# One core, gated mLSTM and routed experts: last heads spread by matmul, q masked for two sequences at a time, and a new order of the routing

## The reference, cut to what matters

```python
def _mlstm_forward(q, k, v, Wi, bi, Wf, bf, ln_scale):
    ...
    log_D = log_fg + jnp.transpose(ig, (0, 1, 3, 2))
    max_log_D = jnp.max(log_D, axis=-1, keepdims=True)
    D = jnp.exp(log_D - max_log_D)
    qk = jnp.einsum('bhsd,bhtd->bhst', qh, kh) / jnp.sqrt(jnp.asarray(dh, q.dtype))
    C = qk * D
    normalizer = jnp.maximum(jnp.abs(C.sum(-1, keepdims=True)), jnp.exp(-max_log_D))
    Cn = C / (normalizer + EPS)
    h = jnp.einsum('bhst,bhtd->bhsd', Cn, vh)
    mu = h.mean(-1, keepdims=True)
    var = ((h - mu) ** 2).mean(-1, keepdims=True)
    hn = (h - mu) * jax.lax.rsqrt(var + EPS)
    hn = hn * ln_scale.reshape(1, nh, 1, dh)
    return hn.transpose(0, 2, 1, 3).reshape(b, s, e)

def _L0_ffn_ref(hidden_states, w_gate, w1, w3, w2):
    logits = x @ w_gate
    logits = SOFTCAP * jnp.tanh(logits / SOFTCAP)
    probs = jax.nn.softmax(logits, axis=-1)
    _, idx = jax.lax.top_k(probs, TOPK)
    mask = jax.nn.one_hot(idx, E, dtype=probs.dtype).sum(-2)
    weights = probs * mask
    for e in range(E):
        h = jax.nn.silu(x @ w1[e]) * (x @ w3[e])
        out = out + h @ w2[e] * weights[:, e:e + 1]

x = x + jnp.tanh(g_xattn[0]) * _L0_xattn_ref(_layernorm(x), ctx, ctx, Wi, bi, Wf, bf, ln_scale)
x = x + jnp.tanh(g_ffn[0]) * _L0_ffn_ref(_layernorm(x), w_gate, w1, w3, w2)
```

## Time and profile before

| | |
|---|---|
| median of 3 runs | 229.91 us (229.88 to 231.53) |
| the profiled execution's own time | 229.46 us |
| its span, first to last instruction | 227.7 us |
| mean granted TensorE clock | 0.956 of full speed |
| PE busy | 197.8 us (87%) |
| VectorE (DVE) busy | 129.8 us (57%) |
| ScalarE (ACT) busy | 111.9 us (49%) |
| GpSimd (POOL) busy | 88.8 us (39%) |

### The profile page before, as it was taken

One profiled execution on the slowest core, in us unless ns is written; L12 is line 12 of the kernel. 1 busy time (PEld: TensorE's weight loads), 2 busy tenths in 40 slices (PEclk: granted clock), 3 DMA queues, 4 the chain that ended last, 5 costly groups with the idle time before them and its releaser, 6 DMA issues.

```text
span 227.7 us, 4241 instructions
## 1 busy us (share of the span) xinstructions
PE 197.8 (87%) x1331; PEld 146.4 (64%) x1332; DVE 129.8 (57%) x310; ACT 111.9 (49%) x224; POOL 88.8 (39%) x96
## 2 busy tenths in 40 slices
PE   8999899898978712769999999999999999999940
PEld 2488544444436511557888888888888888888830
DVE  6897574679899878976777852223323222222310
ACT  2478888898855795026666622233223322223210
POOL 8100343365740000510445646555444555453222
PEclk9999999999999855699999999999999999999997
DMA  3999999901011140210232233333333322334222
GB/s 117 313 367 376 371 373 374 342 24 49 0 49 46 46 153 33 62 33 1 44 53 46 46 49 46 50 55 61 57 58 42 50 46 46 46 52 62 27 23 23
DMA packets 20032, 23.41 MB, mean 103 GB/s; under 512 B 3888, under 2 KB 15152, under 8 KB 20016
## 3 DMA queue, kind: packets, MB, share of 16 engines
q1 hardware_dynamic: 13696, 16.94, 21.6%
q0 software_dynamic: 4464, 6.16, 17.2%
q10 hardware_dynamic: 1856, 0.10, 0.5%
HBM read 17.95 MB, written 5.24 MB: 102 GB/s over the span
## 4 chain that ended last, share of the span: by engine, by line
PE 74%; DVE 12%; ACT 5%; issue 4%; DMA 2%; POOL 1%; DVEq 0%; POOLq 0%; ACTq 0%
PE bank L1335 28%; PE bank L1352 17%; PE bank L1164 6%; PE bank L1061 4%; PE bank L1344 4%; PE bank L1204 3%; ACT arena L487 2%; PE bank L1317 2%; PE bank L1085 2%; DMA out_dram<-hraw,sidx 2%; PE bank L1180 2%; DVE arena L787 1%; DVE vp L968 1%; PE bank L1184 1%; PE bank L1228 1%
## 5 line engine op out<-in xcount | busy, mean ns | idle before, releaser
L447 POOL DMA_INDIRECT out_dram<-hraw,sidx x23 | 37.6, 1636 | 63.1 <-DVE hraw L1021 57.2
L1335 PE MATMUL bank<-arena_r,xn_sb_r 128*128 x184 | 57.2, 392 | 0.0
L1015 DVE TENSOR_TENSOR x_sb<-x_sb,bank 128x512 f32<-128x512 f32 x23 | 15.8, 688 | 57.5 <-ACT x_sb L637 57.5
L1352 PE MATMUL bank<-w_sb,xn_sb 128*128 x184 | 43.6, 380 | 0.8 <-ACT xn_sb L641 0.8
L1335 PEld LDWEIGHTS bank<-arena_r,xn_sb_r 128*128 128x128 f32 x184 | 34.6, 188 | 7.1
L1335 PE MATMUL bank<-w_sb_r,xn_sb_r 128*128 x92 | 38.2, 415 | 0.8 <-issue 0.6
L637 ACT ACTIVATE x_sb<-bank 128x512 f32<-128x512 f32 x23 | 13.7, 598 | 49.5 <-PE bank L1335 49.5
L1352 PEld LDWEIGHTS bank<-w_sb,xn_sb 128*128 128x128 f32 x184 | 33.2, 190 | 4.6 <-issue 1.0
L408 POOL TENSOR_SCALAR_AFFINE_SELECT arena<-arena 128x1024 f32<-128x1024 f32 x16 | 17.7, 1104 | 36.6 <-ACT arena L517 36.6
L641 ACT ACTIVATE xn_sb<-bank 128x512 f32<-128x512 f32 x23 | 13.7, 598 | 25.8 <-PE bank L1344 25.8
L787 DVE TENSOR_TENSOR arena<-bank,arena 128x1024 f32<-128x1024 f32 x16 | 19.6, 1222 | 7.0 <-POOL arena L408 6.8
(11 more groups left out here) (206 smaller groups left out, 257.8 us busy)
## 6 DMA issues: line engine op xcount, KB each, us to landing
w_sb<-in_L_ffn_w_dram SPq DMA_DIRECT2D x24, 512.0 KB, 9.3
x_sb<-in_x_dram SPq DMA_DIRECT2D x2, 512.0 KB, 6.7
arena<-in_ctx_dram SPq DMA_DIRECT2D x2, 512.0 KB, 9.3
out_dram<-x_sb SPq DMA_DIRECT2D x8, 128.0 KB, 1.8
xnorm_scratch<-xn_sb SPq DMA_DIRECT2D x8, 128.0 KB, 1.7
out_dram<-hraw,sidx POOLq DMA_INDIRECT x23, 3.8
cvT<-xnorm_scratch,gidx POOLq DMA_INDIRECT x12
hraw<-xnorm_scratch,gidx POOLq DMA_INDIRECT x11, 2.9
```

What stands on the lines that cost most here:

```text
L447: nc.gpsimd.indirect_dma_start(out=out[:, :], out_offset=bass.IndirectOffsetOnAxis(ap=sidx[:, i:i + 1], axis=0), in_=y_sb[i % 2], in_offse ...
L1335: last = nc.tensor.matmul(ps_scores[p][:, n, :], a, w, start=(k == 0 and j == 0), stop=(k == KC - 1 and j == 2))
L1352: last = nc.tensor.matmul(ps_tr[:, 0:H], hT_sb[p][:, k * P:(k + 1) * P], w2_sb[:, bass.ds(e * W2 + k * H, H)], start=(k == 0), stop=(k == ...
```

## The change

`mask_q` takes two sequences at a time (16 operations on 128 by 512 in place of 32 on 128 by 256), in the even iterations only. For the last two sequences `turn_cv` multiplies with `to_rows` (the identity with `lns` folded in, 17 columns per head without gaps) in place of transposing with the identity; the squares are taken from cvT (`square_last`), and PE sums them over each head with `in_head` (`spread_last`). The top two are looked for in the capped logits and not in their exponentials; the exponentials of the two values found are taken by ScalarE later (`wtop`). Three of the 16 one-hot rows are made by ScalarE, as relu(1 - |slot - i|), VectorE makes the others in two steps. The selectors of weights and the scatter's indices move behind `lower_x(0, 0)`, `slot_weights` behind `split(1)`, the weight table on PE behind the first tile. Warm-ups with other operands are dropped; two and eight of the ordinary kind are added.

```diff
+        LATE_OH = 3
+        SOME = (0, 8, NS - LATE_OH)
+        sqT = dec[:, 0].rearrange("p h s -> p (h s)").rearrange("p (i n) -> p i n", i=2)
...
-            def mask_q(b, heads):
-
-                act.wait_ge(s_qks, Q_STORED[b // 2])
+            def mask_q(seqs, heads):
+
+                act.wait_ge(s_qks, Q_STORED[seqs[-1] // 2])
+                bs = slice(seqs[0], seqs[-1] + 1)
                 for h in heads:
-                    nc.scalar.activation(qm[:, b, :, h, :], qkT[:, b, 0:KC, :], ACT.Copy,
+                    nc.scalar.activation(qm[:, bs, :, h, :], qkT[:, bs, 0:KC, :], ACT.Copy,
                                          scale=pmask[:, h:h + 1]).then_inc(s_qm, 1)
...
+            def square_last(i):
+                act.wait_ge(s_ots, B - 1 + i)
+                nc.scalar.activation(sqT[:, i, :], cvT[:], ACT.Square).then_inc(s_sqT, 1)
...
-                if b + 2 < B:
-                    mask_q(b + 2, (0, 1))
+                if b % 2 == 0 and b + 2 < B:
+                    mask_q((b + 2, b + 3), (0, 1))
...
+                if b >= B - 2:
+                    square_last(b - B + 2)
+                if b % 2 == 0 and b + 2 < B:
+                    mask_q((b + 2, b + 3), (2, 3))
...
-            square_heads(NG - 1)
...
+            act.wait_ge(s_top, 2)
+            nc.scalar.activation(wtop[:], r8[:, 0:TOPK, :], ACT.Exp, scale=SOFTCAP).then_inc(s_exl, 1)
             nc.scalar.preload_act_table_set("silu_and_others")
+            act.wait_ge(s_dump, 16)
+            act.wait_ge(s_slf, 1)
+            for n in range(LATE_OH):
+                follow(nc.scalar.activation(slotd[n % 2], iota_r[:], ACT.Abs, scale=-1.0, bias=slotf[:, n:n + 1]))
+                nc.scalar.activation(oh_r[:, NS - LATE_OH + n, :], slotd[n % 2], ACT.Relu, scale=-1.0,
+                                     bias=one_c[:, 0:1]).then_inc(s_ohl, 1)
...
                     nc.vector.tensor_scalar(lns[:], lns[:], tg[:, 0:1], None, ALU.mult).then_inc(s_par2, 1)
+                    dve.wait_ge(s_par2, 2)
+                    rows = ident.rearrange("p (j v) -> p j v", v=VW)
+                    nc.vector.tensor_reduce(in_head[:], rows[:, :, 0:DH], AX_X, ALU.add).then_inc(s_scl, 1)
+                    nc.vector.tensor_tensor(to_rows[:, :, :, 0:DH],
...
+                    nc.vector.tensor_copy(to_rows[:, :, :, DH:], rows[:, :, DH:DH + 1].unsqueeze(1).to_broadcast(
...
             center_heads(g)
-            spread_heads(g)
+            dve.wait_ge(s_spr, 1)
+            nc.vector.scalar_tensor_tensor(out=rs[:, 0, :], in0=ps_scores[0][:, 0, 0:NH2], scalar=1.0 / DH,
+                                           in1=s16[:, 2, :], op0=ALU.mult, op1=ALU.add).then_inc(s_var, 1)
             stats_x2(g - 1)
+            finish(g)
             aggregate_x2(g - 1)
-            link(nc.vector.tensor_tensor(hh[:], hraw[:, 2 * g % 4:2 * g % 4 + 2, :, 0:DH],
...
-            finish(g)
-            link(nc.vector.tensor_tensor(hflat, hflat, per_head(rs[:, 1, :]), ALU.mult))
+            link(nc.vector.tensor_tensor(hflat, raw_heads(g), per_head(rs[:, 1, :]), ALU.mult))
...
-            lower_weights(0, 1)
...
-            dve.wait_ge(s_exl, 1)
-            src = ex
+            dve.wait_ge(s_th, 1)
+            src = lt
...
+            nc.vector.tensor_copy(slotf[:], sloti[:, 1, NS - LATE_OH:]).then_inc(s_slf, 1)
...
-            for q in range(4):
...
+            for q in range(2):
...
+            lower_weights(0, 1)
             lower_weights(0, 3)
 
+            dve.wait_ge(s_exl, 2)
...
             lower_x(0, 0)
+            token_slots()
+            select_weights()
+            split(1)
             slot_weights()
-            split(1)
             hidden(0, 0)
...
+                    if b < B - 2:
+                        last = nc.tensor.transpose(ps_h[:, g * P:(g + 1) * P], part, ident[:])
+                    else:
+                        last = nc.tensor.matmul(ps_h[:, g * 4 * (DH + 1):(g + 1) * 4 * (DH + 1)], part,
+                                                to_rows[:, g].rearrange("p j v -> p (j v)"), start=True, stop=True)
...
+            def spread_last():
+
+                for i in range(2):
+                    pe.wait_ge(s_sqT, i + 1)
+                    if i == 0:
+                        pe.wait_ge(s_cm, 2 * B)
+                    for g in range(4):
+                        last = nc.tensor.matmul(ps_scores[0][:, 0, i * NH + 4 * g:i * NH + 4 * g + 4],
+                                                sqT[:, i, g * P:(g + 1) * P], in_head[:], start=True, stop=True)
+                last.then_inc(s_spr, 1)
...
+            spread_last()
             turn_x2(1)
             warm_up(4)
...
             turn_x2(3)
+            warm_up(2)
             logits(3)
...
             last.then_inc(s_tab, 1)
+            warm_up(8)
...
-            warm_up(4)
-            warm_up_r(8, 2 * P)
-            warm_up_r(8, P)
             turn_x(0, s_xg[0], 16, 0)
-            weight_table()
             gate_up(0, 0, expert_of(0), 0)
             turn_x(1, s_xg[1], 16, 1, 1)
+            weight_table()
             turn_h(0, 0, False)
```

More of the change, by code:

```diff
@@ L119, in bass_gated_mlstm_moe_kernel @@
         bmask_r = placed("bmask", [P, B])[1]
+        to_rows = sb("to_rows", [P, 4, 4, DH + 1])
+        in_head = sb("in_head", [P, 4])
         tri_s = sb("tri_s", [P, P], BF16)
@@ L173, in bass_gated_mlstm_moe_kernel @@
         etf = sb("etf", [P, NT])
+        slotf = sb("slotf", [P, LATE_OH])
+        wtop = sb("wtop", [P, TOPK, B])
         tab = sb("tab", [P, 5, NT])
@@ L935, in _ @@
                 if k == 0:
-                    link(nc.vector.scalar_tensor_tensor(out=ex2[:], in0=oh[:, 0], scalar=-BIG, in1=ex[:],
+                    link(nc.vector.scalar_tensor_tensor(out=ex2[:], in0=oh[:, 0], scalar=-BIG, in1=lt[:],
                                                         op0=ALU.mult, op1=ALU.add))
@@ L990, in _, with token_slots, select_weights @@
             link(nc.vector.tensor_copy(wpart[:, 2, :], wres[:, 1, :]))
-            for j in range(3):
-                nc.vector.tensor_tensor(wsl[:, :, j, :], sel[:, :, 1, :], nt(wpart[:, j, :]),
-                                        ALU.mult).then_inc(s_wsl, 1)
-            link(nc.vector.tensor_copy(tab[:, 0:2, :].rearrange("p g t -> p (g t)"), ps_small[:, 256:256 + 2 * NT]))
-            link(nc.vector.tensor_scalar(tokf[:, 1, :], tab[:, 1, :], -1.0, 1.0, ALU.mult, ALU.add))
-            link(nc.vector.scalar_tensor_tensor(out=tokf[:, 1, :], in0=tokf[:, 1, :], scalar=dump[:, 0:1],
-                                                in1=tab[:, 0, :], op0=ALU.mult, op1=ALU.add))
-            nc.vector.tensor_copy(sidx[:], tokf[:, 1, :]).then_inc(s_idx, 1)
+            def token_slots():
+                link(nc.vector.tensor_copy(tab[:, 0:2, :].rearrange("p g t -> p (g t)"), ps_small[:, 256:256 + 2 * NT]))
+                link(nc.vector.tensor_scalar(tokf[:, 1, :], tab[:, 1, :], -1.0, 1.0, ALU.mult, ALU.add))
+                link(nc.vector.scalar_tensor_tensor(out=tokf[:, 1, :], in0=tokf[:, 1, :], scalar=dump[:, 0:1],
+                                                    in1=tab[:, 0, :], op0=ALU.mult, op1=ALU.add))
+                nc.vector.tensor_copy(sidx[:], tokf[:, 1, :]).then_inc(s_idx, 1)
+            def select_weights():
+                for j in range(3):
+                    nc.vector.tensor_tensor(wsl[:, :, j, :], sel[:, :, 1, :], nt(wpart[:, j, :]),
+                                            ALU.mult).then_inc(s_wsl, 1)
             def slot_weights():
@@ L1061, in warm_up @@
                     nc.tensor.matmul(ps_ht[:, :], ones_b[:], ones_b[:, :].unsqueeze(1).to_broadcast([P, 4, P]),
-                                     start=True, stop=True)
-            def warm_up_r(n, w):
-                pe.wait_ge(s_wl, 3)
-                for j in range(n):
-                    nc.tensor.matmul(ps_ht[:, 0:w], arena_r[:, j * P:(j + 1) * P], w13_r[:, 0:w],
                                      start=True, stop=True)
```

57 lines of the change are left out of this document (36 added, 21 removed).

## The result

The changed kernel takes 234.01 us (median of 6 runs, 232.12 to 234.44), the kernel before beside it 229.97 (229.52 to 231.53). The ratio is 1.0144, with a 95% interval of 1.0114 to 1.0174: slower, where 227.8 was forecast, with 0.04 for anything above 232.2.

A forecast was written before the change was run, and what follows sets the result against it. PE, busy throughout the expert stage, bounds it, so only that stage's start could move: loop 0, top-two -0.4, slots -0.2, first tile -1.9, between tiles +0.8, together -1.7 from 229.46, so 227.8 us. Range 226.3 to 229.8.

The forecast's parts named there:

- Into the routing: From x2 to the top-two chain: last logits at 1.06 us, full clock; tanh at 80.6, top-two from 80.9, -0.4.
- The bound beside it: Last logits at half clock: logits scaled at 81.0 us, 0.4 later.
- Masks: Wide masks of q in the loop over sequences: even ones 0.24 later, odd 0.28 earlier; counted 0, between -0.2 and +0.1.
- New operands: VectorE building in_head and to_rows at the loop's second product: cost 0, or 0.3 to 0.5 if the floor step waits.
- Last heads: cvT's turn and spread_last on PE: guess of the inverse root at 74.6, x2 at 77.4, 0.7 later than before.
- Top-two and slots: Routing on VectorE: top-two from the tanh, -0.4; one-hot slots and tables, -0.2, gather indices at 90.4.
- From g to the first tile, and between the first two: Gather indices (g) to making the first tile's lower half (S): 4.3, -1.9; S to second tile's matmuls: 7.27, +0.8.
- the 5.65: VectorE's work after the first lower half begins and before the first hidden product, 5.65 us in all.
- The fourth, slower: Eight warm-ups don't lift the clock before the first tile: +2.3 there, 231.5 to 232 in all; chance 0.06.
- The first rival: Clock falls between the first two tiles: second tile costs 1.4 more, 229.2; chance 0.27.
- The third: In the loop a wide mask costs as two narrow ones: +1.8, 229.6; chance 0.07.
- The second, cheaper heads: PE is cheaper in the last heads than counted: x2 0.7 earlier, 226.4; chance 0.15.

The follow-up runs named there:

- e6: The changed kernel with spread_last's matmuls 64 columns wide instead of 4 and the router's logits 64 instead of 8; 228.87 us, ratio 0.9973 to the kernel before.
- e9: e6 with the masks of q as in the kernel before, 32 operations of 256 columns; 229.15 us, ratio 0.9962 to the kernel before.
- e2: The kernel before with the heads part alone: new operands, turn of cvT, spread_last and two warm-ups; 233.22 us, ratio 1.0105.
- e5: The changed kernel with each matmul of spread_last 64 columns wide instead of 4; 231.45 us, ratio 1.0004 to the kernel before.
- e1: The kernel before with the wide masks of q alone; 230.47 us, ratio 1.0022.
- e3: The kernel before with the routing part and the new order of the first tiles alone; 229.37 us, ratio 0.9983.
- e8: e3 with the router's logits 64 columns wide; 227.44 us, ratio 0.9919 to the kernel before.
- e4: The changed kernel with three 512-column warm-ups ahead of spread_last; 233.52 us, ratio 1.0093 to the kernel before.
- e7: The kernel before with the router's logits 64 columns wide; 229.61 us, ratio 0.9993.

## Why the prediction was wrong, point by point

**The step that failed** is in "Into the routing": "with four, three and two warm-ups between the groups PE has hardly a gap there, so I take 1.06". PE had no gap, and the groups took 1.71 to 1.87 all the same. The bound beside it, "at half clock it would be 81.0, 0.4 later", was too small as well: it counted one group slow, but the clock fell ahead of three groups, two turns of x2 and nine warm-ups. The tanh came 3.9 after the forecast 80.6. Of these, 3.12 are the clock (84.52 against e6's 81.40), 0.75 the masks (81.40 against e9's 80.65). What is left, 0.05, is the heads' path: its forecast stands. The shares are good to some 0.2, since e6's loop already ran 0.23 behind the changed kernel's with the same instructions (VectorE's product at 60.17 against 59.93).

**Why the clock falls there.** Shown is that the widths of the sums and logits together bear on it: e6 changes them and not the order, the waits or the work's duration, and its 12 runs have a mean clock of 0.950 or more and at most 230.23 us, while the changed kernel's 6 have 0.943 or less and at least 232.12. Shown too is that it isn't certain: e2 kept the clock in its profiled run with the narrow passes. Not shown is which passes do it. The sums of 4 columns can't be all of it, since in e5's profiled run the clock fell before any of its sums, now wide, was through. And what makes one run of the same kernel keep the clock and another lose it stays open. I argued from waits, as the earlier trace rows offered them (0.89 and 0.69 around 0.66 of work); the trace of before had no such run of narrow passes, and I didn't ask what one would do. The Trainium skill (TensorE: Matmul & The Clock Gate, The HAM clock gate) tells the gate as a matter of how busy PE has been and of its idle gaps. If busy is read as the share of time that PE's instructions cover, this case's trace doesn't agree: 3.56 of 3.56 us covered, and the fall behind it.

**Masks.** "0, between -0.2 and +0.1" was wrong by 0.7. A wide mask takes 0.61 from start to start, not the 0.52 to 0.55 that I took from a plain copy, in the changed kernel's ScalarE and PE timelines:

```profile
44.13 1.32 ACT L503 ACTIVATE arena<-arena,pmask 128x512 f32<-128x512 f32 x2
```

```profile
45.51 1.13 PE L1204 MATMUL bank<-arena 64*128 64x512 f32 x4 [1.08 <-ACT arena L503]
...
50.56 1.13 PE L1204 MATMUL bank<-arena 64*128 64x512 f32 x4
```

PE waits 1.08 instead of 0.66 in every second sequence, at 45.51 and 56.77, and the odd ones, forecast 0.28 earlier, start 50.56 against 50.19: they don't win back what the even ones lose. The nearer row was the mask's own: 0.90 for two of 256 columns. The Trainium skill (ScalarE: Activation LUTs, What ACT_TABLE_LOAD costs) says that an ACTIVATE costs 186 ns and 0.833 ns for a column, and each operand that points to one number per partition 93 more; for a scaled copy of 512 columns that is an estimate of 0.71, and the trace agrees (1.32 for two that overlap, 0.61 apart). e1's profile gives the price apart from the other parts, 0.68 at the last turn of x2, and e9's 0.75 at the tanh.

**New operands.** Right at 0. VectorE's steps start at 31.23, 31.37, 31.70 and 31.79, all ahead of GpSimd's 32.09 as in the earlier trace rows, and none is stretched. At the end of the loop the last products start at 69.27 on PE, and at 69.29 in e1, which has the wide masks and not these operands.

**Last heads.** Right. x2's last step was forecast to end at 77.4; it ends at 77.33 in e2 and at 78.01 in the changed kernel, 0.6 to 0.7 later for the masks. The guess is at 74.42 in e2 (forecast 74.6) and 75.11 here.

**Top-two and slots.** The -0.4 of the top-two chain was not there: 0.46 pass between the tanh's end and the first step (84.78 to 85.24), where I counted 0.05. It isn't a fixed price of the handover from ScalarE: in e3 and e8 the same step starts 0.10 after the tanh's end (81.36 to 81.46, 80.00 to 80.10), though 0.18 then pass before the next step. Why the kernels with the new heads wait longer is open. From there to g it is 9.37, forecast 9.5. Right in the slots, wrong by 0.4 in the handover.

**From g to the first tile, and between the first two.** Right: 4.51 against 4.3, and 7.24 against 7.27 (the five terms of the 5.65 add up to 5.70, which changes nothing). In the profiled run the clock didn't fall there.

**The rivals.** The fourth, slower, named a clock that isn't lifted before the first tile and gave +2.3 for it. It happens, with that price: e4's profile has 9.55 from S to the second tile against 7.24. But it isn't what makes the profiled run slow. It may well be the 2 us by which the four runs at 0.930 to 0.935 stand above the two at 0.942 and 0.943; there is no profile of one of them, so that stays open. The first rival asked about the clock too, between the first two tiles, and the changed kernel's trace shows full clock there. But for the bound of 0.4 on the last logits, all my clock cases stood behind the routing; none stood at the heads, where the change put its new matmuls. The third (masks at +1.8) had the right sign and more than twice the size. The second, cheaper heads, is refuted: `spread_last` takes 1.90.

**What the parts are worth with the clock kept.** e9 against e8 is the heads by matmul alone, and its tanh is 0.91 later (80.65 against 79.74): they cost at least the 0.7 of their path and give nothing back when the logits are wide in both kernels. The routing is worth 2.2 us (e8 against e7), the reordering behind it another 1.3; heads and masks are better left as they were.

## What to carry to other kernels

When matmuls are added to a stretch, look at what PE's passes there are like, not only at its gaps: with passes of 4 and 8 columns this kernel lost 3 us to the clock behind a stretch in which PE was never idle, and with 64 columns for the same results, in nearly the same time, it didn't. Cost a wider instruction from its own narrow form and a rate per column, not from a plainer instruction of the new width. And where runs of one kernel spread, sort them by mean clock before comparing medians: e9 is 0.7 us faster than e6 at equal clock and 0.3 slower by the median.

## What the runs showed of the hardware

- The granted clock fell from 2.4 to 1.2 GHz behind 3.56 us in which PE was busy for 3.56 us, with fp32 passes of 68, 4 and 128 columns and the first warm-up, behind logits of 8; in the profile with 64 columns in place of 4 and 8 it did not (medians 234.01 against 228.87 us). With only the 4 widened it fell in one profile at 71.8 us, 2.5 sooner.
- An fp32 pass of 4 columns and one of 64 took nearly the same time at full clock, some 0.12 us each (1.90 and 1.95 for sixteen).
- The same instructions can meet either clock: e2 ran in 230.0 us at a mean clock of 0.953 and in 234.9 at 0.923.
- VectorE's steps of 32 columns took 1.16 and 1.00 us instead of 0.19 while GpSimd had a sum and a mask of its own. Both steps read two operands from SBUF. The changed kernel's timelines of GpSimd and VectorE:

```profile
62.66 1.27 POOL L435 TENSOR_TENSOR x_sb<-x_sb,hh 128x512 f32<-128x512 f32 x1
62.82 1.16 DVE L852 SCALAR_TENSOR_TENSOR s<-s,floor 128x32 f32<-128x32 f32 x1
63.88 1.10 POOL L423 TENSOR_SCALAR_AFFINE_SELECT arena<-arena 128x1024 f32<-128x1024 f32 x1
64.01 1.00 DVE L854 SCALAR_TENSOR_TENSOR s<-s 128x32 f32<-128x32 f32 x1
```

Each ends within 0.1 us of the GpSimd instruction beside it. In e6, at 72.77 and 73.00, with GpSimd idle, both take 0.19. The Trainium skill (SBUF — State Buffer, Who interferes with whom) says that whoever has the shared ports holds them for the whole instruction, and these rows agree.
